# The last feed-forward of a four-layer kernel: its input normalised inside the first attention, its gated sum and stores inside the last layer, its weights loaded earlier

## What is computed

```python
x = x + tanh(g_xattn[i]) * xattn_i(layernorm(x), ctx, ...)     # i = 0..3
x = x + tanh(g_ffn[i]) * ffn_i(layernorm(x), ...)
```

```python
def _layer(y, wqkv, qs, ksc, wo, lg, lb, w1, b1, w2, b2):
    h = shift_token(y)                       # second half of the features from the token before
    q, k, v = split(h @ wqkv)                # 8 heads of 64
    q, k = rotary_xpos(l2norm(q) * qs, l2norm(k) * ksc)
    y = y + local_attention(q, k, v) @ wo    # causal, within 64 tokens
    h = shift_token(y)
    h = (h - mean) / sqrt(var + 1e-05) * lg + lb
    a, g = split(h @ w1 + b1)                # 2 x 341
    return y + (a * gelu(g)) @ w2 + b2

out = x + tanh(g_ffn[3]) * _layer(_layer(y, ...), ...)
```

## Time and profile before

| what | value |
|---|---|
| median of 3 runs | 3853.03 us (3847.81 to 3855.29) |
| the profiled execution | 3858.39 us, its span 3856.4 us |
| TensorE busy | 3265.1 us, 85% |
| VectorE busy | 2689.2 us, 70% |
| ScalarE busy | 1699.6 us, 44% |
| GpSimd busy | 1182.0 us, 31% |
| mean granted TensorE clock | 0.918 of full speed |

### The profile page before, as it was taken

One profiled execution on the slowest core, in us unless ns is written; L12 is line 12 of the kernel. 1 busy time (PEld: TensorE's weight loads), 2 busy tenths in 40 slices (PEclk: granted clock), 3 DMA queues, 4 the chain that ended last, 5 costly groups with the idle time before them and its releaser, 6 DMA issues. The chain is left out here.

```text
span 3856.4 us, 91767 instructions
## 1 busy us (share of the span) xinstructions
PE 3265.1 (85%) x32139; PEld 2272.1 (59%) x32139; DVE 2689.2 (70%) x5549; ACT 1699.6 (44%) x3176; POOL 1182.0 (31%) x1464
## 2 busy tenths in 40 slices
PE   3687999998888892799859996499997979999876
PEld 1455777877666441666646663266665546666644
DVE  7676655555878779788767767677776547777655
ACT  1333233233777354655412223266664326666521
POOL 1664100001222000144300003177764117777510
PEclk8767999998999896899869998799999989999998
DMA  4211000000000014011100003100000110000011
GB/s 132 66 41 49 0 0 0 0 0 8 13 13 12 1 74 188 24 45 45 35 0 1 0 0 97 35 10 9 9 9 13 30 28 10 8 9 9 3 37 56
DMA packets 163481, 107.86 MB, mean 28 GB/s; under 512 B 91390, under 2 KB 151980, under 8 KB 162348
## 3 DMA queue, kind: packets, MB, share of 16 engines
q1 hardware_dynamic: 161788, 104.02, 9.2%
q10 hardware_dynamic: 1584, 2.44, 0.2%
HBM read 68.52 MB, written 16.78 MB: 22 GB/s over the span
## 5 line engine op out<-in xcount | busy, mean ns | idle before, releaser
L2476 POOL TENSOR_TENSOR la_turned<-la_turned,la_sines 128x1024 f32<-128x1024 f32 x128 | 301.9, 2359 | 142.4 <-DVE la_sines L2402 142.4
L2470 POOL TENSOR_TENSOR la_scaled<-la_turned,la_rlen 128x1024 f32<-128x1024 f32 x128 | 243.7, 1904 | 16.9 <-POOL la_rlen L2463 13.5
L2372 ACT ACTIVATE la_sq<-A 128x1024 f32<-128x1024 f32 x128 | 131.3, 1025 | 105.9 <-PE A L2522 79.5
L916 PE MATMUL B<-l0f_mixed,l0f_sums 128*128 128x256 f32 x768 | 176.2, 379 | 0.0
L2394 DVE TENSOR_TENSOR la_turned<-A,la_cos 128x1024 f32<-128x1024 f32 x128 | 155.5, 1215 | 29.2 <-issue 14.7
L2356 ACT ACTIVATE la_prob<-la_prob 128x512 f32<-128x512 f32 x128 | 80.7, 630 | 205.5 <-DVE la_prob L2415 205.5
L2412 DVE TENSOR_REDUCE la_top<-B 128x8 f32<-128x512 f32 x128 | 88.6, 692 | 108.4 <-PE B L2535 108.4
L2710 ACT ACTIVATE gg_gate<-B,gg_b 128x512 f32<-128x512 f32 (+1 forms) x96 | 65.9, 687 | 211.5 <-PE B L2736 211.5
L916 PEld LDWEIGHTS B<-l0f_mixed,l0f_sums 128*128 128x128 f32 x768 | 145.9, 190 | 19.8
L2407 DVE TENSOR_REDUCE la_length<-la_sq 128x16 f32<-128x1024 f32 x128 | 155.2, 1212 | 0.0
L1386 POOL COPY l1x_vd<-half 128x16 f32<-128x16 f32 x8 | 1.2, 213 | 490.9 <-POOLq L48 490.9
(11 more groups left out here) (467 smaller groups left out, 9287.7 us busy)
## 6 DMA issues: line engine op xcount, KB each, us to landing
l1f_spill<-l1f_work SPq DMA_DIRECT2D x16, 768.0 KB, 3.3
l1f_xT<-l1f_spill SPq DMA_DIRECT2D x16, 768.0 KB, 5.9
l2x_ctx<-in_ctx SPq DMA_DIRECT2D x128, 64.0 KB, 2.2
memory_vd<-vd SPq DMA_DIRECT2D x64, 68.0 KB
X<-in_x SPq DMA_DIRECT2D x4, 1024.0 KB, 6.2
gates_rows<-in_ctx_rows SPq DMA_DIRECT2D x16, 256.0 KB, 2.8
memory_ctxT<-in_ctxT SPq DMA_DIRECT2D x64, 64.0 KB, 1.8
l1x_ctxT<-in_ctxT SPq DMA_DIRECT2D x64, 64.0 KB
```

Source lines behind the costliest of these rows:

```text
L916: last = pe.matmul(bank[:, o * H:o * H + H], weights[:, k, o * P:o * P + P], x[:, k], start=(k == 0), stop=(k == 1))
L2372: act.activation(sq[j % 2][:].rearrange("p n c -> p (n c)"), made[:], ACT.Square).then_inc(squared, 1)
L2470: pool.tensor_tensor(by_head(scaled), by_head(turned), spread_heads(rlen[j % 2][:], W3), ALU.mult)\
L2476: pool.tensor_tensor(turned[j % 2][:], turned[j % 2][:], sines[j % 2][:], ALU.add)\
```

## The change

Four edits, all for `ffn_3`.

1. **Loads.** The weights and tables of `la0`, `gg0`, `la1` and `gg1` get buffers of their own that live from `l2x` on (class `Late`). Their 30 loads are issued at the end of the SyncE stream of `l2x`. The loads at the head of the four stages go.
2. **Input.** The stage `l3f_in` goes. In `la0` VectorE normalises tiles 0 to 3 ahead of its pipeline and one tile in each step after that, eight tiles ahead (`norm_y`); SyncE waits for the tile before it copies it. VectorE's last three turns are written out in place of two.
3. **Output.** The stage `l3f_out` goes. In `gg1` VectorE multiplies `w2` (with the row of b2) by the gate once; GpSimd multiplies each chunk of `y` by the gate and adds it to `m.X`, behind the chunk's power; VectorE's sum then goes to `m.X` and not to `y`.
4. **Stores.** The stage `store` goes. In `gg1` SyncE stores each chunk after its sum, and waits for all 16 stores at the end. For this its loop takes the form of `steps`, in `gg0` too.

```diff
@@ steps4
-def steps4(eng, step, quads=QUADS):
+def steps4(eng, step, quads=QUADS, last=1):
-    with eng.Fori(1, quads - 1) as it:
+    with eng.Fori(1, quads - last) as it:
...
-    for it in (quads - 1, quads):
+    for it in range(quads - last, quads + 1):
@@ attention16, SyncE
                 steps4(sp, step)
+                if not projected:
+                    m.late.load(sp)
@@ local_attention
+        (wq, wk, wv, wo, cos, sin, by, by_swapped), loads = m.late.la[layer]
+        loaded = m.late.la_in[layer]
...
+        normed_y, inputs_seen = st.counter("normed_y", BEFORE), st.sem("inputs_seen")
@@ local_attention, SyncE
-                for tile, src in loads:
-                    sp.dma_start(tile[:], src).then_inc(loaded, 16)
-
                 def shift_in(it, j):
                     t = it * 4 + j
                     sp.wait_ge(h_turned, done(it, j, 4))
+                    if layer == 0:
+                        sp.sem_inc(inputs_seen, 1)
+                        sp.wait_ge(normed_y, done(it, j))
+                        sp.sem_inc(inputs_seen, 1)
                     sp.dma_start(hs[j][:, 0:S], y[:, t, 0:S]).then_inc(h_in[j], 16)
@@ local_attention, VectorE
+                def norm_y(it, j):
+                    t = it * 4 + j
+                    normed(dve, m, y[:, t, :], t).then_inc(normed_y, 1)
...
+                if layer == 0:
+                    for j in range(4):
+                        norm_y(0, j)
                 dve.wait_ge(loaded, 16 * len(loads))
...
                     at4(it, j, -1, outputs)
+                    if layer == 0:
+                        at4(it, j, 8, norm_y)
-                steps4(dve, step)
+                steps4(dve, step, last=2)
@@ new
+class Late:
...
+    def load(self, sp):
+        for layer in range(2):
+            for tile, src in self.la[layer][1]:
+                sp.dma_start(tile, src).then_inc(self.la_in[layer], 16)
+            for tile, src in self.gg[layer][1]:
+                sp.dma_start(tile, src).then_inc(self.gg_in[layer], 16)
@@ gated_gelu
+        last_layer = layer == 1
+        if last_layer:
+            gated_y = st.two("gated_y", [P, TPC, P])
+            w2_gated, stored = st.sem("w2_gated"), st.sem("stored")
+            y_scaled, based = st.sem2("y_scaled"), st.sem2("based")
@@ gated_gelu, SyncE
-                for tile, src in loads:
-                    sp.dma_start(tile, src).then_inc(loaded, 16)
...
+                def store(it, j):
+                    tiles = bass.ds(it * 8 + 4 * j, TPC)
+                    sp.wait_ge(added[j], past(it + 1))
+                    sp.sem_inc(seen, 1)
+                    sp.dma_start(d["out"][:, tiles, :], m.X[:, tiles, :]).then_inc(stored, 16)
+
+                def step(it, j):
+                    at(it, j, 2, shift_in, CHUNK_PAIRS)
+                    if last_layer:
+                        at(it, j, -2, store, CHUNK_PAIRS)
+
+                steps(sp, step, CHUNK_PAIRS)
+                if last_layer:
+                    sp.wait_ge(stored, 16 * NCH)
@@ gated_gelu, VectorE
                     dve.wait_ge(down[j], past(it + 1))
-                    ty = y[:, bass.ds(it * 8 + 4 * j, TPC), :]
+                    if last_layer:
+                        dve.wait_ge(based[j], past(it + 1))
+                    ty = (m.X if last_layer else y)[:, bass.ds(it * 8 + 4 * j, TPC), :]
...
+                if last_layer:
+                    for k, o in ((P, slice(0, F - 1)), (last_k + 1, slice(F - 1, F))):
+                        dve.tensor_scalar(w2[0:k, o], w2[0:k, o], m.tanh_g[0:k, 7:8], None, ALU.mult).then_inc(w2_gated, 1)
@@ gated_gelu, GpSimd
                         pool.tensor_tensor(rstd[j][:], var[j][:], half_power[:], ALU.pow).then_inc(rooted[j], 1)
+                        if last_layer:
+                            tiles = bass.ds(it * 8 + 4 * j, TPC)
+                            pool.wait_ge(based[j], past(it))
+                            pool.tensor_tensor(gated_y[j][:], y[:, tiles, :],
+                                               m.tanh_g[:, 7:8, None].broadcast_to([P, TPC, P]), ALU.mult)\
+                                .then_inc(y_scaled[j], 1)
+                            pool.wait_ge(y_scaled[j], past(it + 1))
+                            pool.sem_inc(pool_seen, 1)
+                            pool.tensor_tensor(m.X[:, tiles, :], m.X[:, tiles, :], gated_y[j][:], ALU.add)\
+                                .then_inc(based[j], 1)
@@ l3_ffn, store and program
-    with Stage(nc, "l3f_in") as st:
...
-    with Stage(nc, "l3f_out") as st:
...
-def store(nc, m, d):
...
+            if n == STAGES.index(l2_xattn):
+                m.late = Late(nc, ctx, d)
```

More of the change, by code:

```diff
@@ L2258, with local_attention_weights @@
 PARTS3 = [(n, min(P, HID3 - n)) for n in range(0, HID3, P)]
+def local_attention_weights(sb, d, layer):
+    G = HEADS3 // 2
+    wq, wk, wv = (sb(n, [P, INNER]) for n in ("wq", "wk", "wv"))
+    wo = sb("wo", [P, G, P])
+    cos, sin = sb("cos", [P, 2, W3]), sb("sin", [P, 2, W3])
+    by, by_swapped = sb("by", [P, 2, W3]), sb("by_swapped", [P, 2, W3])
+    loads = [(wq, d["l3f_wq"][layer]), (wk, d["l3f_wk"][layer]), (wv, d["l3f_wv"][layer]),
+             (wo, d["l3f_wo"][layer]), (cos, d["c_cos"]), (sin, d["c_sin"]), (by, d["l3f_scale"][layer]),
+             (by_swapped, d["l3f_scale_swapped"][layer])]
+    loads = [(tile[:], src) for tile, src in loads]
+    return (wq, wk, wv, wo, cos, sin, by, by_swapped), loads
 def local_attention(nc, m, d, y, layer):
@@ L2588, in _, with gated_gelu_weights, __init__, made_by @@
                 steps4(pe, step)
+def gated_gelu_weights(sb, d, layer):
+    F = len(PARTS3)
+    w1, w2 = sb("w1", [P, 2 * HID3]), sb("w2", [P, F, P])
+    b1 = sb("b1", [P, 2, F])
+    lg, lb = sb("lg", [P, 1]), sb("lb", [P, 1])
+    last_k = PARTS3[-1][1]
+    w2_in = d["l3f_w2"][layer]
+    loads = [(w1[:], d["l3f_w1"][layer]), (w2[:, 0:F - 1], w2_in[:, 0:F - 1]),
+             (w2[0:last_k, F - 1], w2_in[0:last_k, F - 1]), (w2[last_k:last_k + 1, F - 1], d["l3f_b2"][layer]),
+             (b1[:], d["l3f_b1"][layer]), (lg[:], d["l3f_lg"][layer]), (lb[:], d["l3f_lb"][layer])]
+    return (w1, w2, b1, lg, lb), loads
+class Late:
+    def __init__(self, nc, ctx, d):
+        def made_by(weights, name):
+            return [weights(lambda n, shape: ctx.enter_context(nc.sbuf_tensor(f"{name}{layer}_{n}", shape, F32)), d, layer)
+                    for layer in range(2)]
+        self.la, self.gg = made_by(local_attention_weights, "la"), made_by(gated_gelu_weights, "gg")
+        self.la_in, self.gg_in = ([nc.alloc_semaphore(f"late_{n}{layer}") for layer in range(2)] for n in ("la", "gg"))
+    def load(self, sp):
[4 more added lines that the diff above has]
+                sp.dma_start(tile, src).then_inc(self.gg_in[layer], 16)
 def gated_gelu(nc, m, d, y, layer):
@@ L2594, in gated_gelu @@
         F = len(PARTS3)
-        w1, w2 = st.sb("w1", [P, 2 * HID3]), st.sb("w2", [P, F, P])
-        b1 = st.sb("b1", [P, 2, F])
-        lg, lb = st.sb("lg", [P, 1]), st.sb("lb", [P, 1])
         last_k = PARTS3[-1][1]
[L2599 to L2602, removed]
+        (w1, w2, b1, lg, lb), loads = m.late.gg[layer]
+        loaded = m.late.gg_in[layer]
         half_power = st.sb("half_power", [P, TPC])
@@ L2619, in _, with shift_in @@
             def _(sp):
-                for tile, src in loads:
-                    sp.dma_start(tile, src).then_inc(loaded, 16)
                 sp.wait_ge(zeroed, 2)
-                with sp.Fori(0, CHUNK_PAIRS) as it:
-                    for j in range(2):
-                        ty = y[:, bass.ds(it * 8 + 4 * j, TPC), :]
[L2626 to L2629, removed]
+                def shift_in(it, j):
+                    ty = y[:, bass.ds(it * 8 + 4 * j, TPC), :]
+                    sp.wait_ge(normed_h[j], past(it))
+                    sp.sem_inc(seen, 1)
+                    sp.dma_start(hs[j][:, :, 0:S], ty[:, :, 0:S]).then_inc(h_in[j], 16)
+                    for b in range(0, P, S):
+                        sp.dma_start(hs[j][b + 1:b + S, :, S:P], ty[b:b + S - 1, :, S:P]).then_inc(h_in[j], 16)
+                def store(it, j):
+                    tiles = bass.ds(it * 8 + 4 * j, TPC)
+                    sp.wait_ge(added[j], past(it + 1))
+                    sp.sem_inc(seen, 1)
+                    sp.dma_start(d["out"][:, tiles, :], m.X[:, tiles, :]).then_inc(stored, 16)
[6 more added lines that the diff above has]
+                    sp.wait_ge(stored, 16 * NCH)
             @block.vector
@@ L2749, in _ @@
                 pe.wait_ge(loaded, 16 * len(loads))
+                if last_layer:
+                    pe.wait_ge(w2_gated, 2)
                 def step(it, j):
@@ L2834, in program @@
                     stage(nc, m, d, own)
-        store(nc, m, d)
 def l0_xattn(nc, m, d, own):
```

8 lines of the change are left out of this document (4 added, 4 removed).

## The result

The kernel after takes 3804.76 us (median of 4 runs) against 3853.05 us before (4 runs). The ratio is 0.987, with a 95% interval of 0.9853 to 0.9887. That is 48 us less by the medians and 50 by the ratio, where 47 were predicted.

What follows compares the result with a forecast made beforehand. TensorE was taken to bound the loops, so gains lie between stages: 19.1 + 13.9 + 20.4 - 6 = 47.4 us, giving 3806 us against the median of 3853.0. The 8-in-10 range was 3798 to 3819.

Steps and rivals of the forecast that it cites:

- `l3f_in`: Before la0: with the stage gone, la0 begins where it began, 19.1 us won.
- The cover for the normalisations: In la0: SyncE's counters and VectorE's 0.66 us idle before the maximum hide the 64 normalisations; cost 0, at most 16 us.
- Loads: Heads of la0, la1, gg0, gg1: issue times of 3.8, 4.0, 3.2, 3.2 won whole, less 0.3 for counters: 13.9 us.
- That stays: Head of la0: the 3.65 us from the first copy's issue to the first transposition would not change.
- The end: After gg1's last sum: 24.4 us become 4.0 (bounds 3.2 to 4.8), 20.4 us won.
- GpSimd in `gg1`: In gg1: GpSimd's multiplication and sum delay VectorE's normalisations; 0.35 us for 15 chunks plus 0.7 at the start, 6 us lost.
- The start: Start of gg1: GpSimd's new work costs 0.7 us once, where nothing covers it.
- The costlier lock: In gg1: both GpSimd instructions fall whole into normalize, 15 x 1.3 us in place of 5.3; 3820 us, chance 12%.
- No collision: In gg1: GpSimd's sum comes after normalize, or VectorE's four run through; the 6 us stay, 3800 us, chance 13%.
- Loads or stores that are not hidden: Loads hold up l2x's barrier by up to 14 us, or last stores queue, giving 5 back; about 3820 us, chance 6%.
- `norm_y` behind the long instruction: Loop of la0: normalisation falls behind GpSimd's 2.36 us rotation, 1.6 x 60 = 98 us lost; 3904 us, chance 3%.

Runs made afterwards that it cites:

- e2_in_back: Kernel after, with the input stage l3f_in back and no normalisation inside la0: 3822.27 us, ratio 0.9927.
- e1_same: The kernel after, unchanged, run again with a profile: 3807.07 us, ratio 0.9889.
- e3_loads_back: Kernel after, with the 30 loads back at the heads of la0, gg0, la1 and gg1: 3817.30 us, ratio 0.9912.
- e4_out_back: Kernel after, with l3f_out and the single 4 MB store back, and gg1 as gg0: 3816.75 us, ratio 0.9916.
- e7_norm_meets: Kernel after, with la0's norm_y moved within the step to where GpSimd is in its long rotation: 3831.93 us, ratio 0.9953.
- e8_same: The kernel after, unchanged, run again on a third chip: 3804.59 us, ratio 0.9878.
- e5_sum_later: Kernel after, with GpSimd's multiplication and sum in gg1 waiting for VectorE's normalisations of that step: 3798.47 us, ratio 0.9856.
- e9_sum_later: Kernel after, with GpSimd's two instructions of gg1 again behind VectorE's normalisations, on the third chip: 3799.19 us, ratio 0.9864.
- the repeated pair: e8_same and e9_sum_later, compared on one chip: 3804.59 and 3799.19 us.

## Why the prediction was right

**`l3f_in` (19.1 predicted, 19.4 measured).** Right in place and size. The cover for the normalisations was right too. In the loop of `la0` the steps are those of before (7.45, 7.36, 7.45, 7.77 us), and e2_in_back leaves the stage's length unchanged. The normalisation is paid out of VectorE's idle time before the maximum, as forecast. The single step shown does not tell that (0.73 us, where the step of the earlier trace rows had 0.66), but the mean over 380 us of the loop does: 0.79 us before the change and in e2_in_back, 0.53 in e1_same.

**Loads (13.9 predicted; e3_loads_back gives 13.9).** The sum is right, but partly by luck: its parts are off by up to 1.8 us each way. `la0` gained 2.0, not 3.8: SyncE's first copy comes 3.5 sooner behind the memset (5.68 to 2.16), but TensorE's first work only 3.0 (9.33 to 6.32). The normalisations are not what ate the rest, since `la0` is as long without them (e2_in_back). In e3_loads_back, with its loads where they stood before the change, `la0` takes 513.83, 1.2 more than before; so about that much lies in neither loads nor normalisations, and it was not tried. `la1` gained 5.3, not 4.0, but e1_same is its shortest: over the nine profiled executions with early loads it takes 509.60 to 510.89, a gain of 4.0 to 5.3. "That stays", said of the 3.65 us from copy to transposition, failed: they are 4.16, and 3.80 in e2_in_back and 3.70 in e3_loads_back. A head of a stage is a chain of several short waits, and moving one end of it by 3.8 us need not move the other by as much. That the 30 loads stay hidden in `l2x` is shown by SyncE's 22 idle us behind them and by the stage's length.

**The end (20.4 predicted, 21.2 measured).** I took 2.8 us for the store, leaning on the 768 KB write of 3.3. The line through the two transfers gave 2.0, and 2.0 it was. The small terms around it cancel in part: SyncE issues the last store 0.1 us behind the sum, and from its landing to the end it is 1.05 us, where 0.8 was taken. The end of 3.15 us lies just under the stated bounds of 3.2 to 4.8.

**GpSimd in `gg1` (6 predicted, some 6 to 7 measured).** The working held step by step in the loop. The sum starts among the four normalisations and the loser waits for GpSimd's duration less 0.35: predicted 0.91 us for 1.26, measured 2.13 - 1.11 = 1.02 for 1.27. TensorE's slack of 0.8 takes most of it; the first 11 steps are 0.31 to 0.37 us longer than in e4_out_back, where 0.35 was predicted, but the last two are not longer at all, so the sums' span grows by 140.67 - 136.28 = 4.4 us and not by 5.3.

The start is the part that was too small: 0.7 us was predicted. Two blocks of normalisations are late there:

```profile
3637.18 2.83 DVE L2727 TENSOR_SCALAR gg_h<-gg_hs,gg_mean,gg_rstd 128x128 f32<-128x128 f32 x4 [1.23 <-POOL gg_rstd L2774]
...
3654.88 2.30 DVE L2727 TENSOR_SCALAR gg_h<-gg_hs,gg_mean,gg_rstd 128x128 f32<-128x128 f32 x4
```

The first takes 1.7 us more than in e4_out_back, because both the multiplication and the sum hit it, and the third 1.2 more. From the memset to the first sum of `gg1` it is 32.75 us in e1_same and 31.46 to 33.18 in the other runs with this stage unchanged (e2_in_back, e7_norm_meets, e8_same), 30.53 and 30.69 in e5_sum_later and e9_sum_later, and 29.72 in e4_out_back: the start costs about 2 us. The two errors, in the loop and at the start, cancel to within 1 us, so that the total came out near 6 is partly luck. It is 7.4 by e4_out_back, 6.6 by e5_sum_later and 5.9 by the repeated pair.

By the rule of the Trainium skill (SBUF — State Buffer, Who interferes with whom) the loser blocks for the other's whole instruction. The trace agrees with the lock: the third normalisation of the step shown starts 0.01 us behind GpSimd's sum and ends 0.08 us behind its end, and e5_sum_later, which only separates the two in time, brings every one of the 128 instructions back to 348 ns or less. What does not follow is that the block costs VectorE the whole 1.27 us. The normalisation would have taken 0.33 us alone and took 1.34, so 1.0 us was lost. Counting the whole duration made 11 us of the 6, and the measured row was the better base.

**The rivals.** The costlier lock is out, at 0.29 us a step where it needed 1.3. No collision is out as a description, but e5_sum_later makes it true by its wait and measures it: 3798.5 us, where the rival had 3800. Loads or stores that are not hidden: out, by the 22 us behind the loads and the 3.2 us end. `norm_y` behind the long instruction: it did not happen in the loop (median 338 ns), only at the stage's start, where the slowest normalisation of e1_same takes 1539 ns. Its price was overstated, 27 us of the 98, since a short VectorE instruction that comes late in a long one of GpSimd's loses only the rest, and the idle time covered more than half of that. A kernel with it would still be faster than before.

**Left open.** Why `la0` gained 1.8 us less than the loads take to issue. Whether the shorter wait for TensorE at the head of `la0` changes its clock in the first steps was not tried.

## What to carry to other kernels

Work that is moved between stages is priced best at the boundaries: measure from one stage's first instruction to the next one's, before and after, and each edit has its own number, down to about 1 us, even where the medians scatter by more. GpSimd's idle time was not free to use while VectorE's four SBUF-to-SBUF instructions stood in the same place: before GpSimd gets more work, look for what VectorE does at that moment, and put a wait on VectorE's result ahead of it if GpSimd has the time. One such wait gave back the 6 us that the change had lost in `gg1`.

## What the runs showed of the hardware

- A VectorE `tensor_scalar` of 128x128 f32, 0.34 us long, took 1.34 us when a GpSimd sum of 1.27 us started 0.01 us ahead of it, though VectorE's instructions stood back to back: GpSimd got in between two of them. It ended 0.08 us behind GpSimd's instruction, and so did the one that came 0.9 us into a rotation of 2.35 us (e7_norm_meets).
- Putting the same instruction some 3 us earlier in the step (e7_norm_meets) cost 27 us over the stage. What differs is what GpSimd does at the two places: a rotation of 2.35 us at one, small instructions of 0.22 us at the other.
- A store of 256 KB lands in 2.0 us (median of 16, the longest 4.4), one of 4 MB with its closing barrier in 12.0.
